# Token transposes of an attention and mixture-of-experts layer: TensorE against DMA, with the order of the first FFN groups

## What is computed

```python
x = L0_attn_h_t                     # (8, 2048, 1024)
xn = layernorm(x)
x = x + attn(xn) + ffn(xn)          # ffn returns xn + expert_out

# attn: low-rank projections, then 8 heads of 128 + 32
c_q = xn @ W_DQ + b_DQ; c_kv = xn @ W_DKV + b_DKV; k_r = xn @ W_KR + b_KR
attn = softmax(q @ k.T / sqrt(160)); out = (attn @ v_c) @ W_O + b_O

# ffn: Sinkhorn gates over 8 experts, top 2, all experts computed densely
scores = (xn @ router_w.T + router_b) / temp
g = relu(xn @ wg[e]); p = xn @ wp[e]; all_out[e] = (g * p) @ wo[e]
```

## Time and profile before

| what | us |
|---|---|
| median of two runs | 4113.39 |
| the two runs | 4002.54, 4224.25 |
| profiled execution, whole | 3993.38 |
| its span on the slowest core (core 5) | 3991.7 |
| spans of the eight cores | 3948.4 to 3991.7 |
| PE busy in that span | 3626.7 (91%) |
| VectorE, ScalarE, GpSimd busy | 830.1, 743.7, 726.7 |

### The profile page before, as it was taken

How to read it: one execution, slowest core, us unless ns; L and a number is a source line. 1 busy time by engine, 2 the same in 40 slices (tenths; PEclk the granted TensorE clock), 3 DMA queues, 4 the chain that set the end, 5 groups by cost and what they waited for, 6 DMA issues and landing times.

```text
span 3991.7 us, 43638 instructions; the slowest of 8 cores (3948.4 to 3991.7 us)
## 1 busy us (share of the span) xinstructions
PE 3626.7 (91%) x15210; PEld 1467.1 (37%) x15210; DVE 830.1 (21%) x1274; ACT 743.7 (19%) x1211; POOL 726.7 (18%) x1038
## 2 busy tenths in 40 slices
PE   3589999999999999898999989999999999999998
PEld 1233434444443444222222222344444444444443
DVE  3321211112121211122222222212121211211121
ACT  2320101010010101144444443010010101011010
POOL 1012222222222222100000000022222222222221
PEclk8699999999999999878888889999999999999999
DMA  4258778786878788500000000396878779786867
GB/s 74 43 48 111 71 108 85 98 103 81 112 74 114 73 109 92 87 1 1 1 1 1 1 1 0 67 109 75 113 73 113 74 107 100 90 111 72 119 67 134
DMA packets 618343, 290.66 MB, mean 73 GB/s; under 512 B 547340, under 2 KB 547373, under 8 KB 618134
## 3 DMA queue, kind: packets, MB, share of 16 engines
q0 software_dynamic: 610624, 271.03, 57.7%
q1 hardware_dynamic: 7510, 16.86, 1.3%
HBM read 550.39 MB, written 8.39 MB: 140 GB/s over the span
## 4 chain that ended last, share of the span: by engine, by line
PE 84%; DVE 6%; DMA 4%; ACT 3%; issue 3%; DVEq 0%; SPq 0%; POOL 0%; ACTq 0%; POOLq 0%
PE psum L661 22%; PE psum L236 21%; PE psum L244 21%; PE psum L823 4%; PE psum L819 4%; DVE s_resid L683 4%; PE psum L809 3%; PE psum L813 3%; DMA s_areaC<-wexp 3%; PE psum L854 2%; PE psum L711 1%; ACT s_areaB L829 1%; PE psum L461 1%; ACT s_areaB L761 1%; ACT s_areaB L754 1%
## 5 line engine op out<-in xcount | busy, mean ns | idle before, releaser
L236 PE MATMUL psum<-s_xnT,s_wgbuf 128*128 128x512 bf16 x4096 | 984.5, 384 | 47.5 <-DVE s_resid L683 40.3
L661 PE MATMUL psum<-s_areaC,s_areaA 128*128 128x512 bf16 x4096 | 940.1, 390 | 93.7 <-DVE s_resid L683 73.8
L244 PE MATMUL psum<-s_xnT,s_wpbuf 128*128 128x512 bf16 x4096 | 970.2, 380 | 0.0
L255 ACT ACTIVATE s_areaB<-psum 128x512 bf16<-128x512 f32 x512 | 305.7, 597 | 2503.4 <-PE psum L236 2503.2
L187 POOL DMA_DIRECT2D s_wgbuf<-wg x256 | 224.6, 877 | 2354.5 <-PE psum L236 2283.3
L262 DVE TENSOR_TENSOR s_areaA<-s_areaB,psum 128x512 bf16<-128x512 bf16 x512 | 352.3, 688 | 1403.7 <-PE psum L244 1400.7
L661 PEld LDWEIGHTS psum<-s_areaC,s_areaA 128*128 128x128 bf16 x4096 | 404.7, 100 | 626.5 <-issue 179.5
L236 PEld LDWEIGHTS psum<-s_xnT,s_wgbuf 128*128 128x128 bf16 x4096 | 402.1, 99 | 543.6 <-issue 73.9
L244 PEld LDWEIGHTS psum<-s_xnT,s_wpbuf 128*128 128x128 bf16 x4096 | 402.0, 98 | 488.1 <-issue 8.8
L642 POOL DMA_DIRECT2D s_areaC<-wexp x512 | 271.9, 539 | 665.5 <-PE psum L661 663.7
L829 ACT ACTIVATE s_areaB<-psum 128x512 bf16<-128x512 f32 x512 | 305.7, 597 | 431.3 <-PE psum L823 428.9
(11 more groups left out here) (113 smaller groups left out, 708.8 us busy)
## 6 DMA issues: line engine op xcount, KB each, us to landing
s_areaC<-wexp POOLq DMA_DIRECT2D x512, 256.0 KB, 6.9
s_wgbuf<-wg POOLq DMA_DIRECT2D x256, 256.0 KB, 4.5
s_wpbuf<-wp POOLq DMA_DIRECT2D x256, 256.0 KB, 5.6
s_resid<-x SPq DMA_DIRECT2D x16, 512.0 KB, 4.1
y<-s_resid SPq DMA_DIRECT2D x1, 4096.0 KB, 13.5
y<-s_resid SPq DMA_DIRECT2D x2, 2048.0 KB, 7.8
s_areaC<-wo_attn POOLq DMA_DIRECT2D x1, 2048.0 KB, 17.1
s_wcat<-wdq POOLq DMA_DIRECT2D x1, 64.0 KB, 7.1
```

Of the source, the lines that this page charges most:

```text
L236: w.do("tensor", lambda t, c_=c, tb_=tb, tt2_=tt2, gs_=gs, b_=gb: t.matmul(bank(b_)[:, :], S["wgbuf"].ap()[:, gs_, c_, :], S["xnT"].ap()[: ...
L244: w.do("tensor", lambda t, c_=c, tb_=tb, tt2_=tt2, gs_=gs, b_=pbk: t.matmul(bank(b_)[:, :], S["wpbuf"].ap()[:, gs_, c_, :], S["xnT"].ap()[ ...
L255: w.do("scalar", lambda s, b_=gb, sl_=gp_count % 2: s.activation(out=Ebuf[:, sl_, :], in_=bank(b_)[:, :], func=AF.Relu), inc="sS")
L661: w.do("tensor", lambda t, f_=f, dh_=dh, tt_=tt, bk_=bk, ws_=ws, tb_=tb: t.matmul(bank(bk_)[:, :], hbuf[:, f_, tt_ * 128:(tt_ + 1) * 128], ...
```

## The change

Three edits, all in `build_nc`:
- The eight TensorE transposes and eight VectorE copies of a tile become eight DMA transposes (SBUF to SBUF, 128x128 bf16 each) on SP's queue, counted by a new semaphore `qtr`, 16 per transfer. SP waits for the normalised tile and for all transposes of the tiles before; ScalarE waits on `qtr` before it overwrites a slot of `xnbf`; TensorE waits on `qtr` before a block's projections and before the FFN.
- The run-ahead groups in the front stage are gone. The FFN's groups all stand in `do_ffn_tb`, inline, in banks 0 to 3.
- `emit_wgp`, its counters and the body of `emit_gp_group` move behind the gate steps; what they issue for a group is the same.

```diff
-SEM_NAMES = ["qc", "qk", "x0", "x1", "qo",
+SEM_NAMES = ["qc", "qk", "x0", "x1", "qo", "qtr",
...
                     if i >= 2:
-                        w.wait("scalar", "tS", tok[("tr_t", i - 2)])
+                        w.wait("scalar", "qtr", 128 * (i - 1))
...
-                    w.wait("tensor", "sS", tok[("xn_s", i)])
+                    w.wait("sync", "sS", tok[("xn_s", i)])
+                    w.wait("sync", "qtr", 128 * i)
                     for c in range(8):
-                        b = (i * 8 + c) % 2
-                        w.wait("tensor", "vS", bank01[b])
-                        w.do("tensor", lambda t, c_=c, b_=b, sl_=sl: t.transpose(
-                            bankb(b_)[:, 0:128], xnbf[:, sl_, c_ * 128:(c_ + 1) * 128],
-                            S["eyeb"][:]), inc="tS")
-                        tk = w.tok("tS")
-                        w.wait("vector", "tS", tk)
-                        w.do("vector", lambda v, c_=c, b_=b, i_=i: v.tensor_copy(
-                            S["xnT"].ap()[:, c_, i_ * 128:(i_ + 1) * 128], bankb(b_)[:, 0:128]), inc="vS")
-                        bank01[b] = w.tok("vS")
-                        tok[("trev_v", i * 8 + c)] = w.tok("vS")
-                    tok[("tr_t", i)] = w.tok("tS")
+                        w.do("sync", lambda q, c_=c, i_=i, sl_=sl: q.dma_start_transpose(
+                            S["xnT"].ap()[:, c_, i_ * 128:(i_ + 1) * 128],
+                            xnbf[:, sl_, c_ * 128:(c_ + 1) * 128]), inc="qtr", k=16)
...
-                xready = tok[("trev_v", i * 8 + 7)]
+                xready = None
...
-                w.wait("tensor", "vS", xready)
+                w.wait("tensor", "qtr", 128 * (4 * (tn + 1)))
...
-                for _ in range(2):
-                    k = fill_state["k"]
-                    ft_f, tt2_f = k // (TB // 512), k % (TB // 512)
-                    if ft_f >= 16 or tt2_f > B or NTB < 2:
-                        break
-                    emit_gp_group(0, 0, ft_f, tt2_f, fill=True)
-                    fill_state["k"] += 1
...
             def do_ffn_tb(tb, filler=None):
-                rot_state["tb0"] = rot_state["n"]
+                gp_count = gp_state["gp"]
+                tb_gp0 = gp_count
+                w.wait("tensor", "qtr", 128 * NT)
                 for e in range(E):
                     for ft in range(16):
+                        emit_wgp(tb, e, ft)
+                        gs, wgu, wpu = tok[("wgp_slot_of", tb, e, ft)]
                         for tt2 in range(TB // 512):
-                            emit_gp_group(tb, e, ft, tt2)
+                            par = gp_count % 2
+                            gb, pbk = 2 * par, 2 * par + 1
...
```

More of the change, by code:

```diff
@@ L174, in walk @@
             tok = {}
[L175 to L272, removed]
@@ L364, in walk @@
             gidx = 0
-            fill_state = {"k": 0}
             NB = NT // 4
@@ L616, in walk, with emit_wgp @@
             _gs(stepFin)
+            wg_uses = {0: 0, 1: 0, 2: 0}
+            wp_uses = {0: 0, 1: 0, 2: 0}
+            wgp_ci = {"i": 0}
+            wgp_emitted = set()
+            def emit_wgp(tb_, e_, ft_):
+                if (tb_, e_, ft_) in wgp_emitted:
+                    return
+                wgp_emitted.add((tb_, e_, ft_))
+                gs = wgp_ci["i"] % 3
+                wgp_ci["i"] += 1
+                w.wait("gpsimd", "tS", tok.get(("wg_slot_prev", gs)))
+                w.do("gpsimd", lambda q, e2=e_, ft2=ft_, gs2=gs: q.dma_start(
+                    out=S["wgbuf"].ap()[:, gs2, :, :],
+                    in_=dw["wg"][e2, :, :].rearrange("(c p) f -> p c f", p=128)
+                        [:, :, ft2 * 128:(ft2 + 1) * 128]),
+                    inc="wg%d" % gs, k=16)
+                wg_uses[gs] += 1
+                w.wait("gpsimd", "tS", tok.get(("wp_slot_prev", gs)))
+                w.do("gpsimd", lambda q, e2=e_, ft2=ft_, gs2=gs: q.dma_start(
+                    out=S["wpbuf"].ap()[:, gs2, :, :],
+                    in_=dw["wp"][e2, :, :].rearrange("(c p) f -> p c f", p=128)
+                        [:, :, ft2 * 128:(ft2 + 1) * 128]),
+                    inc="wp%d" % gs, k=16)
+                wp_uses[gs] += 1
+                tok[("wgp_slot_of", tb_, e_, ft_)] = (gs, wg_uses[gs], wp_uses[gs])
@@ L619, in walk @@
+            wo_uses = {s: 0 for s in range(8)}
             gp_state = {"gp": 0}
             def do_ffn_tb(tb, filler=None):
-                rot_state["tb0"] = rot_state["n"]
+                gp_count = gp_state["gp"]
+                tb_gp0 = gp_count
+                w.wait("tensor", "qtr", 128 * NT)
                 for e in range(E):
                     for ft in range(16):
+                        emit_wgp(tb, e, ft)
+                        gs, wgu, wpu = tok[("wgp_slot_of", tb, e, ft)]
@@ L625, in do_ffn_tb @@
                         for tt2 in range(TB // 512):
-                            emit_gp_group(tb, e, ft, tt2)
+                            par = gp_count % 2
+                            gb, pbk = 2 * par, 2 * par + 1
+                            needv = max(tok.get(("h_v", gp_count - 2), 0),
+                                        tok.get(("sttb", gb), 0),
+                                        tok.get(("sttb", pbk), 0),
+                                        tok.get("psum_vfree", 0) if gp_count - tb_gp0 < 2 else 0)
@@ new lines, in do_ffn_tb @@
+                            w.wait("tensor", "vS", needv)
+                            w.wait("tensor", "sS", tok.get(("relu_s", gp_count - 2),
+                                                           tok.get("psum_sfree", 0)))
+                            w.wait("tensor", "wg%d" % gs, 16 * wgu)
+                            for c in range(8):
+                                w.do("tensor", lambda t, c_=c, tb_=tb, tt2_=tt2, gs_=gs, b_=gb: t.matmul(
+                                    bank(b_)[:, :], S["wgbuf"].ap()[:, gs_, c_, :],
+                                    S["xnT"].ap()[:, c_, tb_ * TB + tt2_ * 512: tb_ * TB + (tt2_ + 1) * 512],
+                                    start=(c_ == 0), stop=(c_ == 7)),
+                                    inc="tS" if c == 7 else None)
@@ new lines, in do_ffn_tb @@
+                            tok[("g_t", gp_count)] = w.tok("tS")
+                            w.wait("tensor", "wp%d" % gs, 16 * wpu)
+                            for c in range(8):
+                                w.do("tensor", lambda t, c_=c, tb_=tb, tt2_=tt2, gs_=gs, b_=pbk: t.matmul(
+                                    bank(b_)[:, :], S["wpbuf"].ap()[:, gs_, c_, :],
+                                    S["xnT"].ap()[:, c_, tb_ * TB + tt2_ * 512: tb_ * TB + (tt2_ + 1) * 512],
+                                    start=(c_ == 0), stop=(c_ == 7)),
+                                    inc="tS" if c == 7 else None)
@@ new lines, in do_ffn_tb @@
+                            tok[("p_t", gp_count)] = w.tok("tS")
+                            if tt2 == TB // 512 - 1:
+                                tok[("wg_slot_prev", gs)] = tok[("g_t", gp_count)]
+                                tok[("wp_slot_prev", gs)] = tok[("p_t", gp_count)]
+                            w.wait("scalar", "tS", tok[("g_t", gp_count)])
+                            w.wait("scalar", "vS", tok.get(("h_v", gp_count - 2), 0))
+                            w.do("scalar", lambda s, b_=gb, sl_=gp_count % 2: s.activation(
+                                out=Ebuf[:, sl_, :], in_=bank(b_)[:, :], func=AF.Relu), inc="sS")
@@ new lines, in do_ffn_tb @@
+                            tok[("relu_s", gp_count)] = w.tok("sS")
+                            w.wait("vector", "sS", tok[("relu_s", gp_count)])
+                            w.wait("vector", "tS", tok[("p_t", gp_count)])
+                            if gp_count - tb_gp0 < 2 and tok.get("area_a_tfree"):
+                                w.wait("vector", "tS", tok["area_a_tfree"])
+                            w.do("vector", lambda v, b_=pbk, sl_=gp_count % 2, ft_=ft, tt2_=tt2: v.tensor_tensor(
+                                hbuf[:, ft_, tt2_ * 512:(tt2_ + 1) * 512],
+                                Ebuf[:, sl_, :], bank(b_)[:, :], ALU.mult), inc="vS")
@@ L627, in do_ffn_tb @@
+                            tok[("h_v", gp_count)] = w.tok("vS")
+                            tok[("h_ft_v", tb, e, ft)] = w.tok("vS")
+                            tok[("gpbank_v", pbk)] = w.tok("vS")
+                            tok[("gpbank_s", gb)] = tok[("relu_s", gp_count)]
+                            gp_count += 1
                         if filler:
@@ L692, in do_ffn_tb @@
                     tok["bankfree_v"] = tok["stt_prev_v"]
+                gp_state["gp"] = gp_count
             tok["psum_vfree"] = tok["laev_last"]
```

## The result

| | us |
|---|---|
| profiled execution, whole, before and after | 3993.38, 4076.95 |
| span of the slowest core | 3991.7, 4075.4 |
| mean of the eight spans | 3968.9, 4043.5 |
| ratio, after to before | 1.0171, 95% interval 1.0142 to 1.0200 |

The ratio is about 68 us of 3993; its interval ends at 2%. It leaves out executions in which one die's cores ran at a lower granted clock (0.81 to 0.89 against 0.93 in the records); they stand in the recorded median of all 11 runs, 4266.86 us, and so that median is above my range, while the undisturbed runs (4061 to 4086 us) lie inside it.

A forecast was written before the change was run, and what follows sets the result against it. PE, mainly in FFN lines, was 84% of the chain; the change moves only the first 232.6 us. 16 T - 75.7 with T = 11.4 gives +106 on 3993.4, 4100 us; range 4005 to 4250.

The forecast's parts named there:

- Bounds and pieces: Front stage, first 232.6 us: each block's transposes, projections, borrowed groups and next statistics follow one another without overlap.
- Price of the transposes: Front stage, SP queue: eight DMA transposes at 1.02 us plus 3.2 us landing, 11.4 us per token tile.
- Rival A: SP queue: transposes issue at the pace of plain transfers, 4011 to 4023 us; 0.34 together with Rival C's no-change part.
- Rival B: SP queue or DMA engines: each transpose ends before the next starts, 25.6 us per tile, 4327 us; chance 0.10.
- Rival C: Front stage: removing the borrowed groups outweighs the transfers if T is under 4.7 us; over 2% faster given 0.03.
- T: Front stage: time per token tile for its eight DMA transposes, forecast 11.4 us, low 5.8, high 18.3.
- break-even: Front stage: the time per token tile, 4.7 us, at which the transposes' cost equals the 75.7 us saved.
- The borrowed groups: Seven FFN groups run early in the front stage: removal saves 26.7 + 15.5 us, later costs 24.2 + 2.
- Queues, weights, projections: Front stage: x loads behind transposes stay hidden, weights arrive early, projections add nothing, statistics stay 11 us; cost 0.
- the FFN and attention code is otherwise the same: Everything behind the front stage: taken as unchanged, 0 us, so only something outside that stage could give over 2% faster.

The follow-up runs named there:

- e5: Changed kernel with one 128x1024 DMA transpose per token tile in place of eight of 128x128: ratio 0.9859 to the kernel before.
- e6: Changed kernel without SP's wait for the previous tile's transposes, with one counter per slot of the normalised tile: ratio 1.0139 to the kernel before.
- e3: Changed kernel with transposes back on TensorE and copies on VectorE, borrowed groups still removed: profiled execution 3951.57 us, about 0.985 of the kernel before.
- e1: Kernel before the change with its regular FFN groups' bank rotation started one later, banks 2 and 3 first: ratio 0.989, profiled execution 3971.75 us.
- e2: Changed kernel with its FFN groups' bank rotation started in banks 2 and 3: 4124.12 and 4117.98 us, about 1.027 of the kernel before.

## Why the prediction was right or wrong

**Bounds and pieces.** Right. All that the change does directly lies in the first stage, and its pieces follow one another. One reading was wrong and did no harm: block 0 was not at 2.4 GHz. It came to its projections at 1.2 GHz like the others, so its piece had nothing to lose (24 matmuls from 7.0 to 7.6 us per block before, 7.3 to 7.7 after, on the mean of the cores).

**Price of the transposes.** Right in the sum, by two errors that cancel. I put 8 x 1.02 + 3.2 = 11.4 us per tile; it is 7 x 1.275 + 2.4 = 11.3 (11.25 in the chain). The pitch was 20% too low; the landing 0.8 us too high, and it is counted from the start of the issue, so it holds the eighth pitch. The rows of one element per partition (0.92 to 1.12) were nearer than the row with the same bytes (eyeb, 0.42), and that the sum came out within 0.1 us was luck; e5 shows that the rows were near by chance too: the price is not for scattering elements. The Trainium skill (VectorE: DVE Perf Modes, The three transpose paths) states 1309 ns for a 128x128 bf16 through the crossbar; the 1.275 us pitch agrees within 3%. It is a price per instruction in e5: 128x1024 takes 1.22 us of the queue too.

**Rival A.** Wrong. Transposes do not flow like plain transfers when each is 32 KB: 1.23 us of the queue against 0.42 for eyeb with the same 32 KB and 0.33 for an x tile. The rule that stood beside it (the Trainium skill, Advanced Engine Details and Errata, X-Bar Transpose (TRN2): as fast as regular DMAs) does not hold here for eight small ones. For one large no run has a plain transfer of the same size: 256 KB land in 3.1 us, the 512 KB of an x tile in 3.2 to 4.6, and the issue still costs 1.22 us against 0.33.

**Rival B.** Wrong, by the pitch of 1.275 us under a landing of 2.4, and by e6.

**Rival C.** Its condition did not hold in the change, with T at 11.3 us, but its mechanism was sound: e5 brings T to 3.2 us, under the 4.7 of break-even, and 16 x 3.2 - 75.7 is about 24 us less where its first mark comes 23 us earlier. It was larger than I gave it, for the removal of the fill wins outside the stage too. What its sentence left out decided the size of the result.

**The borrowed groups.** Right. My terms (26.7 + 15.5 saved, 24.2 + 2 paid back) gave a gain of 16 us for their removal; e3 has 13.6 in the front stage.

**Queues, weights, projections.** Right. Loads behind the transposes stay hidden, the statistics take 11 us from their first row sum (105.8 to 116.9 us), and the first regular group starts at 317.1 us where I wrote 313.

**The step that failed** is one clause: "the FFN and attention code is otherwise the same", by which the sum put everything behind the front stage at nothing. It is the same code, but the borrowed groups had decided in which banks it starts. The front stage gave +104 us on the mean of the cores against +106 forecast, the FFN -38 against 0. 28 of these are the rotation (e1, where the waits for L683 fall from 40.3 to 16.4 us). With the old rotation put back, e2, the changed kernel comes to about 1.027, 108 us over the kernel before on the same chip: what my sum had. The total is +75 by spans and +68 by the ratio, 1.7% with an interval from 1.4 to 2.0, so slower it is, but within the 2% that I gave 0.34, and not over it, which I gave 0.63. I could have seen it: the page's row for L236 had 40.3 us of waiting for L683, and 32 - 7 = 25 is odd.

Attention's +9 stays open. It does not need the change: from the last FFN matmul of the first half to the first of the second, all eight kernels other than the one before take 7 to 13 us more (e1, which touches nothing ahead of it but the banks, 7), and the clock sum of that stretch goes with it, 115.6 us before, 125.4 after, 124 to 131 in the others. That execution of the kernel before is also the quickest of those listed, by the mean of its spans. Whether that one was merely lucky there the record cannot tell: it holds one profile of the kernel.

## What to carry to other kernels

When an edit removes or adds a few uses of a rotating buffer, follow the rotation past the place of the edit: an odd count moves every later start, and the price (here 1.7 us a time, and a clock that falls after the longer gap) is paid far away. Price small DMA transposes per instruction, and give each as much data as the buffer holds; a loop of eight that is written like the TensorE version pays eight times. Work put "for free" into a stage that is itself on the path is not free, least of all at 1.2 GHz.

## What the runs showed of the hardware

- A DMA transpose on SP costs the queue 1.23 us for 128x128 and 1.22 us for 128x1024 in bf16, SBUF to SBUF, and lands 2.4 and 3.1 us after its issue starts. Several on one queue overlap (a pitch of 1.275 us, or 1.245 with no wait between tiles in e6).
- TensorE idle for 2.9 us between experts was followed by eight matmuls at 1.2 GHz (3.48 us against 1.89) where 1.2 us of idleness was not. It happened behind 60 to 73 of 112 of the longer gaps in three kernels and behind none of 112 of the shorter in each of six. Between variants that differ only in that gap the clock sum of both FFN halves moved by 12 us (before, e1) and by 21 us (after, e2), and their time by 28 and 50 us, 24 of them the gaps.
- Front stages with 47 us of idle TensorE did not make the projections behind them clearly longer (24 matmuls in 7.3 to 7.7 us against 7.0 to 7.6): they began at 1.2 GHz in both kernels, in all four blocks.
- The clock record of a profile can begin late (65.8 us before, 98.3 us after), and a view then shows 1.00 for a stretch whose matmuls take 634 ns and not 379.
